# Epsilon as an extra column of the sums of squares, in place of VectorE's mean-square operation

## The reference

```python
B, T, D, HEADS, DH = 128, 32, 256, 16, 16
rms(v, g) = v * rsqrt(mean(v * v, -1) + 1e-6) * g
scale, shift = split(cond @ W_emb + b_emb)
xn = rms(x, g_norm) * (1 + scale) + shift
q, k, v = heads(xn @ W_qkv)              # 16 heads of 16
q, k = rms(q, g_q), rms(k, g_k)
o = softmax(q @ k.T / 4) @ v             # over the 32 steps of each batch element
x2 = x + o + o @ W_out
# GRU over the 32 steps, from the state h = cond
r = sigmoid(x2_t @ W_ir + b_ir + h @ W_hr + b_hr)
z = sigmoid(x2_t @ W_iz + b_iz + h @ W_hz + b_hz)
n = tanh(x2_t @ W_in + b_in + r * (h @ W_hn + b_hn))
h = (1 - z) * n + z * h
out_t = x2_t + h
```

## Time and profile before

| | |
|---|---|
| median of 3 runs | 372.7 us (371.69 to 374.68) |
| profiled execution | 372.1 us, of which the span of the profile is 370.3 |
| PE busy | 345.9 us (93%), 4334 matmuls |
| DVE busy | 263.2 us (71%), 696 instructions |
| ACT busy | 230.2 us (62%) |
| POOL busy | 206.0 us (56%) |
| chain that ended last | PE 75%, SP's queue 9%, DVE 6%, DMA 4%, issue 4%, ACT 1% |
| granted TensorE clock, mean | 0.983 of full speed |

### The profile page before, as it was taken

The page is one execution under the profiler, slowest core; times in us unless marked ns, Lnnn a source line. Parts: engine busy times, 40 slices in busy tenths (PEclk is TensorE's granted clock), DMA queues, the critical chain, the costliest instruction groups (busy, mean ns, idle before and its releaser), DMA issues.

```text
span 370.3 us, 12367 instructions
## 1 busy us (share of the span) xinstructions
PE 345.9 (93%) x4334; PEld 308.2 (83%) x4334; DVE 263.2 (71%) x696; ACT 230.2 (62%) x668; POOL 206.0 (56%) x384
## 2 busy tenths in 40 slices
PE   8687899999999999999887999999999999999983
PEld 7465788878777887788676999999999999999982
DVE  3566999999999999999975555555555555555553
ACT  4566778777778777876644655556555556555452
POOL 5476777777777777777622444334444444444322
PEclk9898999999999999999998999999999999999998
DMA  6992332322222222223210000000000000000000
GB/s 197 340 315 69 86 85 79 83 79 80 78 71 74 79 79 66 80 79 84 81 39 2 2 30 28 30 28 28 19 9 28 28 28 28 28 28 28 28 31 28
DMA packets 20206, 24.88 MB, mean 67 GB/s; under 512 B 4162, under 2 KB 13012, under 8 KB 20180
## 3 DMA queue, kind: packets, MB, share of 16 engines
q1 hardware_dynamic: 19764, 23.75, 21.1%
q10 hardware_dynamic: 416, 0.79, 0.6%
HBM read 7.48 MB, written 4.19 MB: 32 GB/s over the span
## 4 chain that ended last, share of the span: by engine, by line
PE 75%; SPq 9%; DVE 6%; DMA 4%; issue 4%; ACT 1%; POOLq 0%; POOL 0%; DVEq 0%; ACTq 0%
PE bank L1004 34%; PE bank L1056 21%; PE bank L1150 4%; PE bank L1131 4%; PE bank L1119 4%; SPq L382 3%; PE bank L1111 2%; PE bank L1213 2%; SPq L346 2%; SPq L390 2%; DMA v_diag<-v_rows 2%; PE bank L1102 1%; DMA stage_w<-in_L_cond_W_qkv_dram 1%; DMA operands<-operands 1%; PE bank L1069 1%
## 5 line engine op out<-in xcount | busy, mean ns | idle before, releaser
L1056 PE MATMUL bank<-h,w_hh_sb 128*128 128x128 f32 x768 | 97.1, 275 | 1.5 <-DVE h L992 1.3
L1056 PEld LDWEIGHTS bank<-h,w_hh_sb 128*128 128x128 f32 x768 | 91.2, 191 | 2.3 <-DVE h L992 1.7
L977 DVE SCALAR_TENSOR_TENSOR operands<-bank,vec_cols,operands 128x128 f32<-128x128 f32 x64 | 22.3, 349 | 53.6 <-ACT operands L733 53.5
L733 ACT ACTIVATE operands<-bank,bsum 128x128 f32<-128x128 f32 x64 | 23.5, 367 | 57.2 <-PE bank L1056 53.0
L534 POOL TENSOR_TENSOR operands<-operands,h 128x128 f32<-128x128 f32 x64 | 29.3, 458 | 52.7 <-ACT operands L734 52.7
L1004 PE MATMUL bank<-pair_hi,wih_hi 128*128 128x256 f32 x180 | 52.7, 293 | 0.0
L1004 PE MATMUL bank<-wqkv_hi,xn_hi 128*128 128x256 f32 (+1 forms) x128 | 49.0, 383 | 2.9 <-ACT v_rows L614 2.5
L1004 PE MATMUL bank<-pair_lo,wih_hi 128*128 128x256 f32 x180 | 50.3, 279 | 0.0
L1004 PE MATMUL bank<-pair_hi,wih_lo 128*128 128x256 f32 x180 | 50.2, 279 | 0.0
L541 POOL TENSOR_TENSOR operands<-h,x2T 128x256 f32<-128x256 f32 x32 | 23.2, 725 | 41.3 <-issue 30.3
L1004 PE MATMUL bank<-wqkv_lo,xn_hi 128*128 128x256 f32 (+1 forms) x128 | 43.9, 343 | 0.0
(11 more groups left out here) (118 smaller groups left out, 869.7 us busy)
## 6 DMA issues: line engine op xcount, KB each, us to landing
v_diag<-v_rows SPq DMA_DIRECT2D x128, 34.0 KB, 1.9
operands<-operands SPq DMA_DIRECT2D x64, 64.0 KB, 2.0
operands<-operands SPq DMA_DIRECT2D x32, 128.0 KB, 2.0
out_dram<-operands SPq DMA_DIRECT2D x16, 256.0 KB, 2.0
x_in<-in_x_dram SPq DMA_DIRECT2D x7, 512.0 KB, 9.9
w_hh_sb<-in_L_cond_W_hh_dram SPq DMA_DIRECT2D x1, 768.0 KB, 10.0
stage_w<-in_L_cond_W_ih_dram SPq DMA_DIRECT2D x1, 768.0 KB, 10.9
w_emb_sb<-in_L_cond_W_emb_dram ACTq DMA_DIRECT2D x1, 512.0 KB, 4.6
```

Of the source, the lines that this page charges most:

```text
L733: act.activation(r_g[:, c, :], r_in, ACT.Sigmoid, bias=bsum[:, c:c + 1]).then_inc(r_ready[c], 1)
L977: dve.scalar_tensor_tensor(out=rh[:, c, :], in0=xnh[:, HN_COL:HN_COL + B], scalar=bhh[:, 2 * KC + c:2 * KC + c + 1], in1=r_g[:, c, :], op0 ...
L1056: last = pe.matmul(dst, gate(w_hh_sb, name, c)[k], moving, start=k == 0 and (name == "n" or opens and name == "z"), stop=k == KC - 1, skip ...
```

## The change

The rows of `x_in` and of `square_x` get a 257th element and every head's squares in `square_qk` a 17th. POOL fills these once with constants: in `x_in` one whose scaled square is 4 epsilon, in `square_qk` 4 epsilon itself. The factor 4/16 (and 4/256) goes into the scale of ACT's squares, so that the sums come out as what the mean-square operation made of them. `mean_squares` and its two siblings in the opening are gone, with `ms4` and its semaphore; logarithm and Newton step read the sums, and ACT waits for the sums themselves. The copies of x write 256 of 257 elements of each group. ACT's `input_squares` gets a wait for the Newton step of two turns before, since it now overwrites what that step reads.

```diff
-        x_in = sb("x_in", [P, NG, D])
-        square_x = sb("square_x", [P, D])
+        x_in = sb("x_in", [P, NG, D + 1])
+        square_x = sb("square_x", [P, D + 1])
...
-        square_qk = sb("square_qk", [P, 2 * D])
+        square_qk = sb("square_qk", [P, 2 * HEADS, DH + 1])
...
+SUM_SCALE_X = (4.0 / D) ** 0.5
+SUM_SCALE_QK = (4.0 / DH) ** 0.5
...
-                sp.dma_start(x_in[:, lo:hi, :], x_groups[:, lo:hi, :]).then_inc(loaded, 16)
+                sp.dma_start(x_in[:, lo:hi, 0:D], x_groups[:, lo:hi, :]).then_inc(loaded, 16)
...
+            pool.memset(x_in[:, :, D:D + 1], (4.0 * RMS_EPS) ** 0.5 / SUM_SCALE_X).then_inc(eps_ready, 1)
...
-                pool.tensor_tensor(b, a, ms4[:, nslot, lo:hi], ALU.mult).then_inc(newton_step, 1)
+                pool.tensor_tensor(b, a, ss[:, nslot, lo:hi], ALU.mult).then_inc(newton_step, 1)
...
+            pool.memset(square_qk[:, :, DH:DH + 1], 4.0 * RMS_EPS).then_inc(eps_ready, 1)
...
+            act.wait_ge(eps_ready, 1)
             first_squares(0, FIRST_PAIR)
+            act.wait_ge(ssx_ready, FIRST_PAIR)
+            act.activation(norm_first[:, 2, 0:FIRST_PAIR], norm_first[:, 0, 0:FIRST_PAIR], ACT.Ln)\
+               .then_inc(first_norm, 1)
             act.wait_ge(first_norm, 1)
-            act.activation(norm_first[:, 2, 0:FIRST_PAIR], norm_first[:, 1, 0:FIRST_PAIR], ACT.Ln)\
-               .then_inc(first_norm, 1)
-            act.wait_ge(first_norm, 2)
...
-                act.wait_ge(ms4_ready, n + 1)
-                act.activation(ln_ms[:, nslot, lo:hi], ms4[:, nslot, lo:hi], ACT.Ln).then_inc(ln_ready, 1)
+                act.wait_ge(ssqk_ready, n - LAG_QK + 1)
+                if hi == NS:
+                    act.wait_ge(ssx_ready, n + 1)
+                act.activation(ln_ms[:, nslot, lo:hi], ss[:, nslot, lo:hi], ACT.Ln).then_inc(ln_ready, 1)
...
                 act.wait_ge(ssx_ready, n)
+                act.wait_ge(rs_ready, n - 1)
                 act.sem_inc(square_x_free, 1)
-                act.activation(square_x[:, :], x_in[:, n, :], ACT.Square, scale=(DH / D) ** 0.5,
+                act.activation(square_x[:, :], x_in[:, n, :], ACT.Square, scale=SUM_SCALE_X,
...
-                act.activation(square_qk[:, :], p_qk[slot][:, :], ACT.Square).then_inc(sq_ready, 1)
+                if isinstance(g, int) and g == 0:
+                    act.wait_ge(eps_ready, 2)
+                act.activation(square_qk[:, :, 0:DH], p_qk[slot][:, :].rearrange("p (h d) -> p h d", d=DH), ACT.Square,
+                               scale=SUM_SCALE_QK).then_inc(sq_ready, 1)
...
-            dve.wait_ge(ssx_ready, FIRST_PAIR)
-            dve.tensor_scalar(norm_first[:, 1, 0:FIRST_PAIR], norm_first[:, 0, 0:FIRST_PAIR], 4.0 / DH,
-                              4.0 * RMS_EPS, ALU.mult, ALU.add).then_inc(first_norm, 1)
...
-                dve.tensor_reduce(ss[:, nslot, 0:2 * HEADS], square_qk[:, :].rearrange("p (h d) -> p h d", d=DH),
+                dve.tensor_reduce(ss[:, nslot, 0:2 * HEADS], square_qk[:, :, :],
                                   AX_X, ALU.add).then_inc(ssqk_ready, 1)
-
-            def mean_squares(n, nslot):
-                lo, hi = norm_columns(n)
-                dve.wait_ge(ssqk_ready, n - LAG_QK + 1)
-                if hi == NS:
-                    dve.wait_ge(ssx_ready, n + 1)
-                dve.tensor_scalar(ms4[:, nslot, lo:hi], ss[:, nslot, lo:hi], 4.0 / DH, 4.0 * RMS_EPS,
-                                  ALU.mult, ALU.add).then_inc(ms4_ready, 1)
...
-                n = norm_item(base, u, 0)
-                if n is not None:
-                    mean_squares(n, u % 2)
```

More of the change, by code:

```diff
@@ L102, in adaptive_attention_gru @@
         NS = 2 * HEADS + 1
-        square_qk = sb("square_qk", [P, 2 * D])
+        square_qk = sb("square_qk", [P, 2 * HEADS, DH + 1])
         ss = sb("ss", [P, 2, NS])
-        ms4 = sb("ms4", [P, 2, NS])
         threes = sb("threes", [P, NS])
@@ L184, in adaptive_attention_gru @@
         ones_ready = sem("ones_ready")
+        eps_ready = sem("eps_ready")
         wqk_hi_ready = sem("wqk_hi_ready")
@@ L202, in adaptive_attention_gru @@
         ssqk_ready = sem("ssqk_ready")
-        ms4_ready = sem("ms4_ready")
         ln_ready = sem("ln_ready")
@@ L497, in _ @@
             first = [norm_first[:, i, 0:FIRST_PAIR] for i in range(7)]
+            pool.wait_ge(first_norm, 2)
+            pool.tensor_tensor(first[4], first[3], first[3], ALU.mult).then_inc(first_norm, 1)
             pool.wait_ge(first_norm, 3)
-            pool.tensor_tensor(first[4], first[3], first[3], ALU.mult).then_inc(first_norm, 1)
+            pool.tensor_tensor(first[5], first[4], first[0], ALU.mult).then_inc(first_norm, 1)
             pool.wait_ge(first_norm, 4)
-            pool.tensor_tensor(first[5], first[4], first[1], ALU.mult).then_inc(first_norm, 1)
+            pool.tensor_tensor(first[4], threes[:, 0:FIRST_PAIR], first[5], ALU.subtract).then_inc(first_norm, 1)
             pool.wait_ge(first_norm, 5)
-            pool.tensor_tensor(first[4], threes[:, 0:FIRST_PAIR], first[5], ALU.subtract).then_inc(first_norm, 1)
-            pool.wait_ge(first_norm, 6)
             pool.tensor_tensor(first[6], first[4], first[3], ALU.mult).then_inc(first_norm, 1)
@@ L511, in second_norms @@
                 pool.wait_ge(newton_step, LAG_QK)
-                pool.tensor_tensor(second[5], second[4], second[1], ALU.mult).then_inc(newton_step, LAG_QK)
+                pool.tensor_tensor(second[5], second[4], second[0], ALU.mult).then_inc(newton_step, LAG_QK)
                 pool.wait_ge(newton_step, 2 * LAG_QK)
@@ L585, in second_norms @@
                 second = slice(FIRST_PAIR, FIRST_NORMED)
-                act.wait_ge(ms4_ready, LAG_QK)
-                act.activation(norm_first[:, 2, second], norm_first[:, 1, second], ACT.Ln).then_inc(ln_ready, LAG_QK)
+                act.wait_ge(ssx_ready, FIRST_NORMED)
+                act.activation(norm_first[:, 2, second], norm_first[:, 0, second], ACT.Ln).then_inc(ln_ready, LAG_QK)
                 act.wait_ge(ln_ready, LAG_QK)
@@ L663, in scaled_input @@
                 if first and n < FIRST_PAIR:
-                    act.wait_ge(first_norm, 7)
+                    act.wait_ge(first_norm, 6)
                 else:
@@ L669, in scaled_input @@
                 act.sem_inc(xhat_free, 1)
-                act.activation(xhat[:, slot, :], x_in[:, n, :], ACT.Copy,
+                act.activation(xhat[:, slot, :], x_in[:, n, 0:D], ACT.Copy,
                                scale=norm_first[:, 6, n:n + 1] if first else rs[:, slot, NS - 1:NS])\
@@ L896, in residual @@
                     dve.wait_ge(x2T_ps, o - 1)
-                dve.tensor_tensor(x2[:, slot, :], p_w, x_in[:, o, :], ALU.add).then_inc(x2_ready, 1)
+                dve.tensor_tensor(x2[:, slot, :], p_w, x_in[:, o, 0:D], ALU.add).then_inc(x2_ready, 1)
             def probs_transposed(g, slot):
@@ L944, in body @@
                     modulation()
-                if turn_is(base, u, DVE_XMOD):
-                    second_norms()
                 if turn_is(base, u, DVE_XMOD + 1):
```

## The result

The changed kernel takes 367.42 us (median of 20 runs, 364.95 to 370.91), the kernel before 372.65 (median of 20). The ratio is 0.988, 95% interval 0.986 to 0.991: 1.2% faster. The profiled execution took 367.0 us, its span 364.9 against 370.3. The ratios here leave out the runs that took over 1.5% more than the fastest of their kernel, and they are not the quotients of the medians (0.986 here).

A forecast was written before the change was run, and what follows sets the result against it. DVE was taken as the bound from about 71 us, with PE 0.25 us per turn behind; 4.4 + 0 + 0.5 + 0 - 0.3 = 4.6 us off 372.1 gave 367.5 us, range 365.8 to 371.0.

The forecast's parts named there:

- the steady part: Attention from 71 us, 19 turns at PE's 5.06 us: 96.4 instead of 100.8 us, 4.4 gained, bounds 3.9 and 4.8.
- x_in: Loads of x into rows off 32-byte boundaries: a loss of 0.3 us taken; 0 at ratio 1, 11.8 at a doubling.
- the tail: From 172.67 us, SP's last copies begin earlier because DVE's xmod is on time: 0.5 us gained, bounds 0 and 0.8.
- DVE was the bound: In the steady attention DVE sets the turn at about 5.30 us; relief helps only until PE's own 5.06.
- The price of the operation: Removing the mean square from DVE's steady turn saves 0.76 us, longer sums add 0.04: 5.30 becomes 4.58 us.
- The loop's branch: PE's branch every four steady turns: between 0 and 0.10 us each, taken as 0.06 x 5 = 0.3 us.
- The head: The turns from 46 to 71 us, PE already at 5.06 in its best: 0 gained, bounds 0 and 0.4.
- the cover: The v_rows starting at 30.01 wait for a copy, hiding the opening's gain; without it some 0.5 us would count.
- the opening: ACT's first logarithms no longer go through DVE: some tenths of a microsecond per pair, 0 reaching the end.
- The rival of slower loads: Loads of x a quarter slower per row cost 2.9 us, total 370.1; chance 0.12 somewhat slower, 0.07 losing.
- Another cycle: Rival: an exchange among PE, ACT, DVE and POOL holds the steady turn at 5.18 us, total 369.5; chance 0.12.
- the signs: Expected in the changed profile: DVE busy about 84 of 93 us, sums about 0.70 us, loads landing in 9.9 us.

The follow-up runs named there:

- experiments 9: The kernel before with four products a turn cut from PE (input's low part left out of values and output projection): 372.35 us, ratio 1.000.
- experiment 10: The changed kernel with four products a turn cut from PE (input's low part left out of values and output projection): 360.53 us, ratio 0.965.
- The spare operation: The changed kernel with an unused tensor_scalar on ss put back in the removed operation's place in DVE's queue: 370.20 us, ratio 0.994.
- experiments 2 and 4: The kernel before with only x_in's padding: 372.71 us, ratio 1.001; the kernel before with only the opening's part of the change: 372.12 us, 1.001.
- experiment 11: The changed kernel with ACT issuing some v_rows copies instead of SP, for groups 0 to 6 and 28 to 31: 367.40 us, ratio 0.988.
- experiment 12: The changed kernel with ACT issuing some v_rows copies instead of SP, for groups 28 to 31 alone: 369.65 us, ratio 0.993.
- experiment 7: The changed kernel with an unused tensor_reduce over one element of ss in the removed operation's place on DVE: 368.37 us, ratio 0.991.

## Why the prediction was right

The forecast was 367.5 us and the measured median is 367.42; that close a hit is partly luck: the steady part gave 0.4 us more than forecast, x_in cost 0.3 less, the GRU added 1.3 that no term holds, the tail took 1.2 more, and two sets of runs differ by 1.4.

- **DVE was the bound, and PE's pace the limit behind it.** Shown from both sides by experiments 9 and 10, and by 5.05 us in the loop against the 5.06 read off the chain.
- **The price of the operation.** 0.76 us from start to start, hold included, and 0.04 for the longer sums: the forecast 4.58 for DVE's turn is 4.57 in experiment 10, and the transpose follows the sums after 0.62 against 0.63. Had the price been the operation's own 0.18 us, DVE's turn would be 5.30 - 0.18 + 0.04 = 5.16, still above PE's pace, and the 19 turns would have gained some 2 us less. The spare operation shows what made the step expensive: lying behind POOL's work in each turn.
- **The steady part.** 4.8 us in 19 turns where I said 4.4, at the upper bound. The loop's branch, for which I took 0.3, costs nothing visible. The bounds 3.9 and 4.8 don't follow from the terms that I gave for them: 100.8 - 96.1 is 4.7, and 0.10 us for each of five branches less is 4.2.
- **The head.** 0 forecast, 0.0 measured at the 9th scores, in this pair; executions differ there by 3.5 us, so that exact a hit is luck. SP's issuing still sets it, PE's scores waiting for copies of keys, but the wait of v_rows at 30.01, which I called the cover, was 1.00 us instead of 3.93, outside the 0.5 us that I allowed for its start.
- **The tail.** Mis-sized, and of the other sign: 0.5 gained was forecast, 0.7 was lost. The step itself came (the keys 0.3 us earlier than the scores of that time), but the copies behind it landed up to a microsecond late. The term took their landing time as fixed.
- **x_in and the opening.** 0.3 us was set aside, 0 was measured (experiments 2 and 4), with 1.8 us as the most that the interval leaves. The rival of slower loads falls at its 2.9 us.
- **Another cycle.** Not there; DVE's idle 0.31 us at xmod is the slack I put at 0.4. Of the signs, DVE's busy time was mis-sized: 86.4 of 93 us from 71 to 164, where I said 84; the sums took 0.70 us, as said, and the loads landed in 9.5 us at the median, near the 9.9 said. At 4.58 us a turn PE and DVE meet, and the next gain needs both.
- Not in the sum at all: 1.3 us of the profiled difference, the clock granted in the GRU.

## What to carry to other kernels

When two engines are nearly full, find which one the other waits for at the turn's boundary, and read the other's unbroken turn off the chain: the difference of the two turns is all that any relief of the first can give, and a cut of the second's work, tried on both kernels, shows it. Price an operation by start to start in its queue, not by its shortest run, and look at what runs on POOL beside it. If it is held there, changing its kind or its source may do as much as removing it: a spare `tensor_reduce`, or a spare `tensor_scalar` from PSUM without its wait, cost nothing here that four turns or the time show.

## What I hadn't expected

- An operation of 32 columns takes 0.18 us or 0.70 to 0.77 us by whether it begins 0.02 us ahead of a POOL operation or with it. Whether one wait more ahead of it can decide that is open.
- SP's seven copies a turn take 4.2 us in the middle of its loop (2.41 + 1.78). Before 70 us, in the turns written out as in the loop's first ones, SP starts a turn's copies 4.4 to 5.6 us after those of the turn before: in about every second turn one issue takes 1.2 to 1.6 us instead of 0.59. Why is open.
- Two idle times of PE of 1.1 to 1.4 us within 4 us, near the end of the attention, were followed by the lower clock: 0.62 and 0.53 over 8 us in experiment 11, 0.57 over 4 us in experiment 12. In experiment 7 it followed one of 1.89 us; one of 2.23 us in the changed kernel wasn't followed by it.
- Two sets of runs of the same kernel against the same other one gave 0.988 and 0.994, with 95% intervals that just miss each other; the quotients of their medians are 0.986 and 0.990.
